# Attention output packed two heads to 32 rows before the output projection, output bias added to the residual on GpSimd

## The reference, cut to what matters

```python
q = jnp.einsum('bsd,dhf->bshf', inputs_q, Wq) + bq
k = jnp.einsum('bsd,dhf->bshf', inputs_kv, Wk) + bk
v = jnp.einsum('bsd,dhf->bshf', inputs_kv, Wv) + bv
q = q / jnp.sqrt(jnp.asarray(HEAD_DIM, q.dtype))
attn = jnp.einsum('bqhf,bkhf->bhqk', q, k)
attn = jax.nn.softmax(attn, axis=-1)
ctx = jnp.einsum('bhqk,bkhf->bqhf', attn, v)
out = jnp.einsum('bqhf,hfd->bqd', ctx, Wo) + bo
...
x = _layernorm(x + out)
```

## Time and profile before

| | us |
|---|---|
| median of 3 runs | 1689.43 |
| lowest, highest | 1685.65, 1699.95 |
| the profiled execution | 1687.66 |
| its span in the trace | 1685.9 |
| PE busy | 1361.7 (81%) |
| DVE busy | 1466.5 (87%) |
| ACT busy | 1113.7 (66%) |
| GpSimd busy | 902.0 (54%) |

### The profile page before, as it was taken

One profiled execution on the slowest core, in us unless ns is written; L12 is line 12 of the kernel. 1 busy time (PEld: TensorE's weight loads), 2 busy tenths in 40 slices (PEclk: granted clock), 3 DMA queues, 4 the chain that ended last, 5 costly groups with the idle time before them and its releaser, 6 DMA issues. The chain is left out here.

```text
span 1685.9 us, 22891 instructions
## 1 busy us (share of the span) xinstructions
PE 1361.7 (81%) x7612; PEld 959.2 (57%) x7612; DVE 1466.5 (87%) x2714; ACT 1113.7 (66%) x2452; POOL 902.0 (54%) x659
## 2 busy tenths in 40 slices
PE   7687778778877877787877879988998899889880
PEld 5566566656666666566665645456545654464460
DVE  5999999999999999999999956597859785978678
ACT  5877887788788778877887523337633763375570
POOL 1778877787878788788778600002800280028015
PEclk9889889888988998998898989999999999999995
DMA  7200210221022022102111021100020001000000
GB/s 237 67 26 32 69 68 3 70 70 42 28 70 70 1 69 70 58 13 70 64 33 56 13 86 46 40 1 1 11 70 1 1 14 38 1 1 1 25 1 25
DMA packets 38040, 70.02 MB, mean 42 GB/s; under 512 B 3553, under 2 KB 31682, under 8 KB 33698
## 3 DMA queue, kind: packets, MB, share of 16 engines
q1 hardware_dynamic: 37922, 68.56, 12.1%
HBM read 59.90 MB, written 8.65 MB: 41 GB/s over the span
## 5 line engine op out<-in xcount | busy, mean ns | idle before, releaser
L900 POOL TENSOR_TENSOR state_c<-state,c_area 128x1024 f32<-128x1024 f32 x256 | 601.7, 2361 | 168.2 <-DVE state L970 149.0
L970 DVE TENSOR_TENSOR_SCAN state<-decay,ps 128x512 f32<-128x512 f32 x512 | 620.5, 1212 | 0.0
L686 ACT ACTIVATE decay<-step_area,negA 128x255 f32<-128x255 f32 x1024 | 432.5, 496 | 0.5 <-DVE step_area L1049 0.5
L945 DVE TENSOR_TENSOR ps<-step_area,ps 128x512 f32<-128x512 f32 x512 | 349.7, 683 | 10.6 <-PE ps L368 8.5
L1562 POOL TENSOR_TENSOR big<-big,g_sb 128x1024 f32<-128x1024 f32 x29 | 80.8, 2788 | 504.8 <-ACT big L1462 502.8
L384 PE MATMUL ps<-ident_sb,state_c 128*128 128x128 f32 x2048 | 294.8, 292 | 12.6 <-POOL state_c L900 12.5
L384 PEld LDWEIGHTS ps<-ident_sb,state_c 128*128 128x128 f32 x2048 | 255.5, 151 | 40.7 <-POOL state_c L900 23.0
L368 PE MATMUL ps<-parts,sel_bc_sb 96*128 96x256 bf16 x256 | 75.4, 295 | 95.8 <-DVE ps L961 75.8
L1421 PE MATMUL ps<-w_sb,hT 128*128 128x256 f32 x512 | 119.9, 388 | 2.4 <-ACT hT L1531 1.9
L1386 PE MATMUL ps<-w_sb,weights 128*128 128x512 f32 x256 | 121.0, 608 | 0.1
L1650 DVE BATCH_NORM_STATS2 stats<-big 128x6 f32<-128x256 f32 x256 | 88.4, 414 | 28.1 <-ACT big L1536 20.2
(11 more groups left out here) (210 smaller groups left out, 2386.6 us busy)
## 6 DMA issues: line engine op xcount, KB each, us to landing
c_area<-c_scratch SPq DMA_DIRECT2D x32, 1024.0 KB, 6.4
weights<-in_xT SPq DMA_DIRECT2D x16, 256.0 KB, 3.0
res<-in_x SPq DMA_DIRECT2D x16, 256.0 KB, 2.8
x_scratch<-res SPq DMA_DIRECT2D x16, 256.0 KB, 8.2
weights<-x_scratch SPq DMA_DIRECT2D x4, 1024.0 KB, 7.8
xa<-x_scratch SPq DMA_DIRECT2D x4, 1024.0 KB, 5.4
out_x<-acc SPq DMA_DIRECT2D x4, 1024.0 KB, 4.4
w_sb<-in_w SPq DMA_DIRECT2D x2, 1024.0 KB, 13.8
```

The costliest lines, as they stand in the source:

```text
L686: nc.scalar.activation(decay[:, n % RING, j, 1:], dt_sb[:, i[1] % 2, j, 1:], ACT.Exp, scale=negA[:, j * NS + n:j * NS + n + 1]).then_inc(s ...
L900: nc.gpsimd.tensor_tensor(state_c[:, n % RING, :, :], state[:, n % RING, :, :], c_bc[:, q, n, :].unsqueeze(1).to_broadcast([P, CT, TC]), A ...
L945: nc.vector.tensor_tensor(bu_ps[m % 3][:, :].rearrange("p (j n) -> p j n", j=2), u_sb[:, i[1] % 2, 2 * h:2 * h + 2, :], b_ps[n % 2][:, 0:T ...
L970: nc.vector.tensor_tensor_scan(state[:, n % RING, pair, :].rearrange("p j n -> p (j n)"), decay[:, n % RING, pair, :].rearrange("p j n -> ...
```

## The change

The division now writes only the 16 channels of each block, into a tile `packed` in which the even groups take the first and the odd groups the second 16 of each 32 columns. The transpose back into `oT` is done once for two groups, and `oT` and `wo` have 2 groups of 128 full rows. The projection does 16 products instead of 32. The bias row is gone from `wo`; instead GpSimd adds `bo` to `xa`, one 128x2048 addition for each image: for image 0 at the start, for image `b + 1` once image `b` is normalised (`s_x2`) and the new `xa` is loaded. DVE's additions to the residual wait for that (`s_xb`). `raw` has one buffer instead of two. A load of `bo` is added at the start of the second half.

```diff
@@ tiles and semaphores
-        raw = sb("raw", [P, 2, HALF])
+        raw = sb("raw", [P, HALF])
+        packed = sb("packed", [P, NL, HALF])
+        bo_sb = sb("bo_sb", [P, DM])
...
+        s_xb = sem("a_xb")
+        s_bo = sem("a_bo")
@@ SP, start
             load_x1(0, xa[:, :, :], s_x)
+            sp.dma_start(bo_sb[:, :], bo.partition_broadcast(P)).then_inc(s_bo, 16)
@@ PE, project
                     for g in groups:
                         last = nc.tensor.matmul(ps[:, t % 4, 0:DM], oT[:, g, t * P:(t + 1) * P], wo_sb[:, g, :],
-                                                start=g == 0, stop=g == G - 1)
-                    if g == G - 1:
+                                                start=g == 0, stop=g == G // 2 - 1)
+                    if g == G // 2 - 1:
                         last.then_inc(s_proj, 1)
...
-                pe.wait_ge(s_o, b * U + U - 3)
+                pe.wait_ge(s_o, b * U // 2 + 1)
                 for t in range(TG):
-                    project(t, range(G - 1))
-                pe.wait_ge(s_o, b * U + U - 1)
+                    project(t, [0])
+                pe.wait_ge(s_o, b * U // 2 + 3)
                 for t in range(TG):
-                    project(t, [G - 1])
-                pe.wait_ge(s_o, b * U + U)
+                    project(t, [1])
+                pe.wait_ge(s_o, b * U // 2 + 4)
                 for t in range(TG, TT):
                     pe.wait_ge(s_r, b * TT + t - 3)
-                    project(t, range(G))
+                    project(t, range(G // 2))
@@ GpSimd
+            def residual(b):
+
+                pool.wait_ge(s_x, b * 16 + 16)
+                nc.gpsimd.tensor_tensor(xa[:, :, :], xa[:, :, :], bo_sb[:, :].unsqueeze(1).to_broadcast([P, TT, DM]),
+                                        ALU.add).then_inc(s_xb, 1)
+
+            pool.wait_ge(s_bo, 16)
+            residual(0)
             pool.wait_ge(s_const, LOADS * 16)
 
             def turn(b, more, tail):
+                if more:
+                    pool.wait_ge(s_x2, b * TT + TT)
+                    residual(b + 1)
@@ DVE, attend
-                    blocks = raw[:, u % 2, :].rearrange("p (k c) -> p k c", c=BLK)
+                    blocks = raw[:, :].rearrange("p (k c) -> p k c", c=BLK)
+                    mine = packed[:, half, :].rearrange("p (k s c) -> p k s c", s=2, c=HD)[:, :, g % 2, :]
                     dve.wait_ge(s_pv, b * U + u + 1)
-                    if u >= 2:
-                        dve.wait_ge(s_o, b * U + u - 1)
-                    nc.vector.transpose(raw[:, u % 2, :], ps[:, 5 + u % 2, :]).then_inc(s_raw, 1)
-                    dve.wait_ge(s_raw, b * U + u + 1)
                     if u:
                         dve.wait_ge(s_div, b * U + u)
+                    nc.vector.transpose(raw[:, :], ps[:, 5 + u % 2, :]).then_inc(s_raw, 1)
+                    dve.wait_ge(s_raw, b * U + u + 1)
                     nc.vector.reciprocal(inv[:, :], blocks[:, :, HD]).then_inc(s_inv, 1)
                     dve.wait_ge(s_inv, b * U + u + 1)
-                    nc.vector.tensor_tensor(blocks, blocks, inv[:, :].unsqueeze(2).to_broadcast([P, HALF // BLK, BLK]),
+                    nc.vector.tensor_tensor(mine, blocks[:, :, 0:HD], inv[:, :].unsqueeze(2).to_broadcast([P, HALF // BLK, HD]),
                                             ALU.mult).then_inc(s_div, 1)
-                    dve.wait_ge(s_div, b * U + u + 1)
-                    nc.vector.transpose(oT[:, g, half * HALF:(half + 1) * HALF], raw[:, u % 2, :]).then_inc(s_o, 1)
+                    if g % 2:
+                        dve.wait_ge(s_div, b * U + u + 1)
+                        nc.vector.transpose(oT[:, g // 2, half * HALF:(half + 1) * HALF], packed[:, half, :]).then_inc(s_o, 1)
@@ DVE, residual
-                dve.wait_ge(s_x, b * 16 + 16)
+                dve.wait_ge(s_xb, b + 1)
@@ shapes and data
-        late["qT"], late["oT"] = views(c_area, (G, L), (G, L))
+        late["qT"], late["oT"] = views(c_area, (G, L), (G // 2, L))
...
-                ("wo", [P, G, DM], channels(wo)), ("w1", [P, KT, E * DM], channels(w1)),
+                ("wo", [P, G // 2, DM], channels(wo)), ("w1", [P, KT, E * DM], channels(w1)),
...
-    wo = np.zeros((NH, BLK, DM), f32)
-    wo[:, :HD] = xatt("Wo")
-    wo[0, HD] = xatt("bo")
+    wo = xatt("Wo").reshape(G // 2, 2, HG, HD, DM).transpose(0, 2, 1, 3, 4)
```

More of the change, by code:

```diff
@@ L1063, in _, with attn_ffn_block @@
             round_neg(1)
-def attn_ffn_block(nc, x1, ctxT, ident_sb, w, ps, late, shared, g2, be2, bias_rows, before, out):
+def attn_ffn_block(nc, x1, ctxT, ident_sb, w, ps, late, shared, bo, g2, be2, bias_rows, before, out):
     U = G * NL
@@ L1863, in _, with decoder_block @@
             last_tail(BATCH - 1)
-def decoder_block(nc, x, xT, w_in, w_x, w_out, par, ident, sel_bc, sel_p, ctxT, wq, wk, wv, wo, bqk, bv,
+def decoder_block(nc, x, xT, w_in, w_x, w_out, par, ident, sel_bc, sel_p, ctxT, wq, wk, wv, wo, bo, bqk, bv,
                   w1, w2, gw, gb, lnp, bias_rows, g2, be2, before, out):
@@ L1917, in decoder_block @@
                     shared, w, ctxT)
-        attn_ffn_block(nc, x1, ctxT, ident_sb, w, ps, late, shared, g2, be2, bias_rows, before, out)
+        attn_ffn_block(nc, x1, ctxT, ident_sb, w, ps, late, shared, bo, g2, be2, bias_rows, before, out)
 def _constants():
@@ L1963, in _layout @@
         ctxT=np.asarray(inputs["ctx_1024"]).reshape(BATCH * S, DM).T,
-        wq=heads(xatt("Wq")), wk=heads(xatt("Wk")), wv=heads(xatt("Wv")), wo=wo.reshape(NH * BLK, DM),
+        wq=heads(xatt("Wq")), wk=heads(xatt("Wk")), wv=heads(xatt("Wv")), wo=wo.reshape(NH * HD, DM), bo=xatt("bo"),
         bqk=np.concatenate([heads(xatt("bq")).reshape(G, P).T, heads(xatt("bk"), 1).reshape(G, P).T], 1),
@@ L1973 @@
 _ARGS = ["x", "xT", "w_in", "w_x", "w_out", "par", "ident", "sel_bc", "sel_p", "ctxT", "wq", "wk", "wv", "wo",
-         "bqk", "bv", "w1", "w2", "gw", "gb", "lnp", "bias_rows", "g2", "be2", "before"]
+         "bo", "bqk", "bv", "w1", "w2", "gw", "gb", "lnp", "bias_rows", "g2", "be2", "before"]
 def kernel(**inputs):
```

## The result

| | before | changed |
|---|---|---|
| median of 20 runs, us | 1692.25 | 1683.51 |
| lowest, highest | 1685.65, 1700.82 | 1675.18, 1688.36 |
| profiled execution, its span | 1687.66, 1685.9 | 1675.18, 1673.4 |

The ratio of the runs is 0.9941, 95% interval 0.9923 to 0.9959: about 10 us faster (7 to 13). The forecast was 14.0 us and 1673.7, with a range of 1667 to 1682, and the median lies 1.5 us above that range. PE's and DVE's parts went as forecast. What did not is the clock of PE behind image 3's normalisations, which the sum put at nothing, and the base from which the gain was taken off.

The account below looks back on a forecast made before the run. DVE's tile pace, not PE, was taken to bound the tails, PE image 0. Gains of 6.8, 2.2, 2.2 and 2.8 for images 0 to 3 made 14.0 us; 1687.66 less that gave 1673.7 us, range 1667 to 1682.

Parts of the forecast that it names:

- Projection: PE's projection in each image: 16 products fewer save 7.0 us, 28.0 over four images as upper bound.
- Image 0: Image 0 has no tail: 7.0 us gain less handshakes, 6.8 us, with GpSimd's addition just fitting.
- Division: DVE's division of 256 instead of 512 elements: 0.42 us instead of 0.69, runs of 16 costing nothing extra.
- The last unit meets GpSimd: Tails: division meets GpSimd's multiplication or slips between instructions; additions start at 1208.3, `aggregate` at 1217.4, 2.8 us earlier.
- GpSimd's addition: GpSimd's 128x2048 bias addition takes 4.5 us, bounds 4.2 and 9, beside DVE's key copies behind the normalisations.
- Copies: DVE's four SBUF-to-SBUF key copies, 0.92 us together, at worst wait about 3.7 us for GpSimd's addition.
- the worst end: For DVE's key copies, the forecast assumed the full wait of about 3.7 us rather than passing beside GpSimd.
- rows 8: Profile rows cited for the copies: SBUF-to-SBUF `TENSOR_SCALAR` waited beside GpSimd, 0.878 against 0.409 us, 2.442 at worst.
- Images 1 and 2: Gain 2.2 us each; of 7.0 us off PE, 3.2 lost to DVE's tile pace, 1.6 to GpSimd's addition.
- Image 3: Last image: nothing follows but DVE's `aggregate`, so the gain is 2.8 us.
- rival 4: New pause before keys in images 1 and 2 drops PE's clock, 13.3 us lost each: 1700.3 us; chance 0.05.
- The base: Gain subtracted from the one profiled execution, 1687.66 us, noted as 1.8 below the median of runs shown.

Follow-up runs that it names:

- experiment 5: Kernel before with only 2 of its 4 groups projected, old division, all transposes and no GpSimd addition; ratio to before 0.9932.
- experiment 6: Changed kernel with each projection product issued twice, so PE again spends 14.0 us on the projection; ratio to before 0.9994.
- the late addition: Changed kernel with GpSimd's addition for the next image waiting for that image's first four reductions instead of the normalisations; ratio to before 0.9919.
- late statistics: Kernel of the late addition, also numbered 9, with the previous image's eight statistics moved behind the eight projection additions; ratio to before 0.9906.
- experiment 3: Changed kernel with 10 unused 128x512 products filling PE's pause before image 3's transposes; ratio to before 0.9917.
- experiment 8: Changed kernel with 3 unused filling products in image 3, making PE's pause 6.39 us; ratio to before 0.9945.
- experiment 2: Changed kernel without GpSimd's bias addition, semaphore raised at the same place; ratios to before 0.9889 and, run again, 0.9937.
- experiment 4: Changed kernel run again unaltered for a second trace; ratio to before 0.9948, second half 673.7 us.

## Why the prediction was wrong, and where right

Point by point, by its own steps:

- *Projection*: 7.10 us in image 0, forecast 7.0. Image 0 gained 6.9, forecast 6.8. In the tails it stretched to 8.8, forecast about 9. Right.
- *Division*: 0.424 us at its shortest, forecast 0.42. Runs of 16 elements cost nothing extra. The old length of 0.69 does not come out of the rows that the prediction names (2.72 less 2.17 of waiting is 0.55), but the shortest old division in the trace did take 0.691.
- *The last unit meets GpSimd*: additions start at 1199.62, which is 1208.72 with the 9.10 us added; forecast 1208.3. `aggregate` at 1217.68, forecast 1217.4, and GpSimd's tail ended at 1216.7, as forecast. Right. Experiments 5 and 6 show what carries it: PE's shorter work gives 1.4 us of the 2.8, DVE's shorter unit the other 1.4, and the latter only together with PE's.
- *GpSimd's addition*: 4.51 us, forecast 4.5.
- *Copies*: held, one of 3.97 us in image 2 (forecast 3.9) and one of 4.52 in image 1; the worst end was the right one to take, and rows 8 the right neighbours. The Trainium skill, page "SBUF — State Buffer", section "Who interferes with whom", has it that an SBUF-to-SBUF copy can take the ports that DVE shares with GpSimd, and that whoever issues first then blocks the other for the whole instruction; the trace agrees, with 4.52 us for the copy that met the addition against 0.206 for one that did not.
- *Images 1 and 2*: 2.2 each forecast, 1.8 and 2.3 gained by the schedule (1.8 because the load of `xa` landed 6.6 us after its issue instead of 5.4, behind the normalisations, and the addition started late). Near, and for the forecast reasons: of the 7.0 us off PE, 3.2 were to be lost to DVE's tile pace and 1.6 to the addition; the late addition gave back 1.66 and 1.11, and late statistics 2.3.
- *Image 3*, "Nothing follows but DVE's `aggregate`, so 2.8": this step failed. Up to the gate the schedule gave 2.5, and 2.3 of it were lost from the gate on, where PE worked at 1.2 GHz for another 4.9 us; with the pause filled the loss was gone (experiment 3). The prediction knew the row of it but priced the clock at one place only, ahead of the keys in images 1 and 2 (rival 4), where PE paused 1.56 us and the granted clock stayed at 1.00. It never asked what the clock does in the place where it was already seen low, when everything ahead of it moves. A further 0.9 us went the same way in image 1's experts, and neither was in the sum, which put the clock at 0: 14.0 forecast, 10.3 in the traces.
- *The base*, "1687.66 - 14.0": this step failed as well. The one profiled execution had a first half of 1001.65 us; in the traces of this study it runs from 999 to 1014, and the median of 20 runs of before is 1692.25, 4.6 above the profiled one. Three runs from 1685.65 to 1699.95 showed that width; the prediction named 1.8 us of it. With the gain as forecast and the better base the number is 1678, inside the range; with the measured gain and the old base 1677, inside too. Both together are 1682.0, at the edge, and the run gave 1683.5.

What stays open is what sets the two ends of the stretch at 1.2 GHz. The table of experiment 8 shows that its place, against the work behind the pause, goes with the loss. It is not the length of the pause (experiments 2, 8 and 9), nor, in two traces of two, chance between runs of one kernel (experiment 4). Why the clock came back 3 us after the start of the transposes in some schedules and 9 us after it in others, with the same transposes and gate to do, no run here shows.

## What to carry to other kernels

Halving one engine's work in a stretch buys what the next engine leaves: look for its pace per tile (here 1.1 us of DVE against 1.75 of PE) and for what its idle time was hiding, because a collision that is hidden before comes onto the path when the other side gets faster. Put work of GpSimd where DVE waits, not where DVE copies from SBUF to SBUF; the same addition cost 2.8 us beside the copies and nothing where DVE waited for the gate. Before subtracting a gain from one execution, ask how much the untouched part varies, and where PE's clock is already seen low, give that place its own term with both signs.

## What was not expected of the hardware

How long the granted clock stayed low behind a pause did not follow the pause's length, and it repeated in both traces of one kernel: after image 3's pause the same instructions took 31.1 or 33.4 us, and once 32.69 us (experiment 5), and the last segment of image 1 took 37.9 to 38.2 or 39.0 to 39.3. The first half, in which the kernels differ by one load at most, took 999.3 to 1014.1 us. Two executions of one kernel can differ by more than this whole change is worth: the twenty of the changed kernel lie between 1675.18 and 1688.36 us.
